# Nine-tap convolution by five products for three outputs in place of four for two, with the first pair's residual rows kept in DRAM

## What is computed

```python
def conv1d_same(x, w, b): ...          # padding SAME along the 748 tokens
rc = conv1d_same(gelu(conv1d_same(xt, rc_w1, rc_b1)), rc_w2, rc_b2)   # router scores, top 2 of 10 experts
y  = ...                               # chosen experts' outputs, weighted by gates
sh = silu(conv1d_same(xt, sh_w1, sh_b1))   # 128 -> 512 channels, NINE taps
sh = conv1d_same(sh, sh_w2, sh_b2)         # 512 -> 128, one tap
z  = residual + y + sh
out = h + layer_norm(z, ln_g, ln_b)
```

## Time and profile before

| | us |
|---|---|
| median of 3 runs | 1531.79 (1531.74 to 1535.3) |
| the profiled execution | 1544.43 |
| its span, first to last instruction | 1542.6 |
| attention, iteration 0 (no convolution), start of `h3` to end of `scores` | 571.5 to 686.6 |
| iterations 1, 2, 3 | 160.8, 163.6, 166.3 |
| the tail, to the first matmul of `experts1` | 1177.3 to 1267.6 |
| PE busy over the span | 1305.9 (85%) |
| the convolution's product matmuls (L1133) | 261.6 busy, 1536 instructions |

### The profile page before, as it was taken

One profiled execution on the slowest core, in us unless ns is written; L12 is line 12 of the kernel. 1 busy time (PEld: TensorE's weight loads), 2 busy tenths in 40 slices (PEclk: granted clock), 3 DMA queues, 4 the chain that ended last, 5 costly groups with the idle time before them and its releaser, 6 DMA issues.

```text
span 1542.6 us, 33397 instructions
## 1 busy us (share of the span) xinstructions
PE 1305.9 (85%) x10360; PEld 1103.2 (72%) x10361; DVE 1003.6 (65%) x3235; ACT 644.9 (42%) x1610; POOL 699.3 (45%) x1055
## 2 busy tenths in 40 slices
PE   6696777787899937778899899988998989999974
PEld 3464646564899935556788778876887989999953
DVE  4467768665466656757863786467663628989946
ACT  1346272523122204335335453445334436666623
POOL 0112556444688853133531444242614526777732
PEclk9697989898999978989999899999998999999987
DMA  6000400003588840010010001000100237777725
GB/s 191 4 21 6 111 27 22 25 21 95 161 266 256 263 170 1 2 42 1 24 61 0 2 14 58 14 1 1 43 1 8 95 97 191 196 194 198 196 88 161
DMA packets 102202, 128.46 MB, mean 83 GB/s; under 512 B 21015, under 2 KB 61181, under 8 KB 101842
## 3 DMA queue, kind: packets, MB, share of 16 engines
q1 hardware_dynamic: 88786, 102.36, 23.1%
...
## 4 chain that ended last, share of the span: by engine, by line
PE 60%; DVE 15%; issue 7%; DVEq 6%; POOL 5%; ACT 4%; DMA 2%; POOLq 0%; SPq 0%; ACTq 0%
PE psum L980 12%; PE psum L1133 11%; PE psum L989 9%; DVE work L1554 3%; PE psum L1142 3%; PE psum L1047 2%; POOL rows_in L2130 2%; PE psum L1094 2%; PE psum L1072 2%; PE psum L794 2%; PE psum L1191 2%; PE psum L969 2%; PE psum L1018 2%; DVE stats L1537 2%; PE psum L1067 1%
## 5 line engine op out<-in xcount | busy, mean ns | idle before, releaser
L1133 PE MATMUL psum<-NT,wreg 128*128 128x182 f32 (+1 forms) x1536 | 261.6, 326 | 10.2 <-ACT pack L1434 5.1
L1133 PEld LDWEIGHTS psum<-NT,wreg 128*128 128x128 f32 x1536 | 247.9, 192 | 18.9 <-ACT pack L1434 5.9
L2162 POOL DMA_INDIRECT rows_out<-work,expert_row_kept x208 | 206.2, 992 | 79.6 <-issue 41.1
L980 PE MATMUL psum<-work 128*128 128x128 f32 x1664 | 222.7, 277 | 0.9 <-ACT work L1336 0.9
L980 PEld LDWEIGHTS psum<-work 128*128 128x128 f32 x1664 | 203.9, 193 | 1.7 <-issue 0.9
L2111 POOL TENSOR_TENSOR rstd<-var_eps,pack 128x6 f32<-128x6 f32 x40 | 56.5, 1415 | 215.0 <-DVE var_eps L1544 214.9
L1329 ACT ACTIVATE work<-psum,work 128x128 f32<-128x128 f32 x416 | 118.6, 368 | 64.4 <-PE psum L980 64.3
L1876 DVE SCALAR_TENSOR_TENSOR work<-psum,work 128x128 f32<-128x128 f32 x416 | 117.1, 344 | 7.7
L794 PE MATMUL psum<-pack,work 128*128 128x128 f32 (+2 forms) x288 | 51.4, 336 | 82.0 <-DVE work L1554 75.5
L1885 DVE TENSOR_SCALAR work<-psum,expert_row_kept 128x128 f32<-128x128 f32 x208 | 72.8, 350 | 71.8 <-PE psum L969 36.6
L2130 POOL DMA_INDIRECT rows_in<-N,slot_now x96 | 100.5, 1046 | 28.6 <-issue 28.4
(11 more groups left out here) (364 smaller groups left out, 2894.3 us busy)
## 6 DMA issues: line engine op xcount, KB each, us to landing
...
```

Source lines behind the costliest of these rows:

```text
L980: r_ = mm(v.ps1[:, c * P:(c + 1) * P], v.w1[:, c * P:(c + 1) * P], v.xT, start=True, stop=True)
L1133: r = mm(bank[:, half * HALF_PAIRS:half * HALF_PAIRS + p1 - p0], weights[:, m * P:(m + 1) * P], product_input(name, g, k, p0, p1), start=( ...
L2162: G.indirect_dma_start(rows_out[m], bass.IndirectOffsetOnAxis(ap=v.dest, axis=0), v.y, None, bounds_check=last, oob_is_err=False).then_inc ...
```

## The change

Three neighbouring outputs of a group now come from five products (points 0 to 4). A unit is a *whole* lane and a block `m`: 250 triples, so 15 matmuls of 250 columns in three fills, `p12` (6), `p03` (6), `p4` (3), where there were 24 matmuls of 192 and 182 columns. The two PSUM banks alternate from fill to fill. DVE joins with 7 operations over 250 columns, SiLU takes 748 columns at once. The four blocks' outputs of a lane no longer fit into their old place: blocks 2 and 3 lie in `H` over the first pair's residual rows, which SP writes to DRAM in iteration 0 and brings back after the second experts' loads. `ln_b` is therefore added earlier, in steps of their own (`add_ln_b`), between `turn(0)` and `add_b_sh2(0)`; `add_b_sh2` adds to `N` alone. `rows` of a lane's two halves now come together: those of lane 0 behind the first unit of lane 1, those of lane 1 both in `CONV_END`. `turn` has 12 additions in place of 3, `make_conv_weights` 8 in place of 3. The weights come by four DMAs in place of two, the same bytes.

```diff
+        CONV_POINTS = 5
+        conv_w = wreg[:, 0:CONV_POINTS * 3 * 512].rearrange("p (x g c) -> p x g c", x=CONV_POINTS, g=3)
...
+        conv_h = [conv_h_own[:, m, :] for m in range(2)] + [
+            H[:, m * TILES:(m + 1) * TILES, :].rearrange("p j d -> p (j d)") for m in range(2)]
+        first_rows = H[:, 0:LANES * TILES, :].rearrange("p j d -> p (j d)")
...
-        for u, (q, m) in enumerate(UNIT):
-            PARTS.append(("bc", q, m))
-            if m == 1 and q > 0:
-                PARTS.append(("rows", q - 1, 0))
-            PARTS.append(("ad", q, m))
-        CONV_END = [("last", UNITS - 1, 3), ("rows", UNITS - 1, 0)]
...
+        for k, m in UNIT:
+            PARTS += [(x, k, m) for x in POINTS]
+            if m == 0 and k > 0:
+                PARTS += [("rows", 2 * k - 2, 0), ("rows", 2 * k - 1, 0)]
+        CONV_END = [("last", LANES - 1, 3), ("rows", UNITS - 2, 0), ("rows", UNITS - 1, 0)]
+        COST = {"p12": 6, "p03": 6, "p4": 3, "rows": 4}
...
+            sp.wait_ge(first_rows_final, 1)
+            sp.dma_start(first_rows_dram, first_rows).then_inc(first_rows_out, 16)
...
+            sp.wait_ge(pe_conv_done, pe_conv.end("conv")[0][1])
+            sp.wait_ge(first_rows_out, 16)
+            sp.dma_start(first_rows, first_rows_dram).then_inc(first_rows_back, 16)
...
+                    for half, x in enumerate(POINTS[what]):
                         for g in range(3):
-                            weights = {"a": conv_taps[:, g, 0], "b": conv_taps[:, g, 1], "c": conv_c[:, g], "d": conv_taps[:, g, 2]}[name]
-                            r = mm(bank[:, half * HALF_PAIRS:half * HALF_PAIRS + p1 - p0], weights[:, m * P:(m + 1) * P],
-                                   product_input(name, g, k, p0, p1), start=(g == 0), stop=(g == 2))
-                    r.then_inc(pe_conv_done, pe_conv.step("conv", f"{what}{m}_{q}", 0))
-                elif what == "rows":
-                    e.wait_ge(act_conv_done, act_conv.at("conv", f"s3_{q}", 0, i))
-                    for j in range(3):
-                        n_ = WIDTH[3 * (q % 2) + j]
-                        acc = conv_bank[1][0:n_, j * P:(j + 1) * P]
-                        for m in range(4):
-                            r = mm(acc, conv_h[:, m, j * P:j * P + n_], conv2[:, m * P:(m + 1) * P], start=(m == 0), stop=(m == 3))
-                    r.then_inc(pe_conv_done, pe_conv.step("conv", f"rows0_{q}", 0))
+                            r = mm(bank[:, half * TRIPLES:(half + 1) * TRIPLES], conv_w[:, x, g, k_cols(m)], turned(k)[:, x, g:g + TRIPLES],
...
+                bk, bm, bi = unit_before(k, m, i, 2 if what == "p12" else 1)
+                e.wait_ge(dve_conv_done, dve_conv.at("conv", f"y{bm}_{bk}", 0, bi))
+                dst = {"p12": conv_p12[u % 2], "p03": conv_p03, "p4": conv_p4}[what]
...
-                V.tensor_tensor(conv_sum[:, 0:n_], b, c, ALU.add)
-                V.tensor_tensor(b, b, c, ALU.subtract)
...
-                V.scalar_tensor_tensor(y[:, 0], conv_sum[:, 0:n_], 0.5, a, ALU.mult, ALU.add)
-                V.scalar_tensor_tensor(y[:, 1], b, 0.5, d_, ALU.mult, ALU.subtract
...
+                if u == 2:
+                    e.wait_ge(first_rows_out, 16)
+                e.wait_ge(act_conv_done, act_conv.at("conv", f"p4{m}_{k}", 0, i))
+                V.scalar_tensor_tensor(conv_sum, p1, 3.0, p2, ALU.mult, ALU.add)
+                V.scalar_tensor_tensor(p2, p1, -3.0, p2, ALU.mult, ALU.add)
+                V.scalar_tensor_tensor(p0, p0, 3.0, p3, ALU.mult, ALU.add)
+                V.scalar_tensor_tensor(conv_p4, conv_p4, 1.5, p3, ALU.mult, ALU.add)
                 e.drain()
-                V.scalar_tensor_tensor(y[:, 0], conv_sum[:, 0:n_], 0.5, a, ALU.mult, ALU.add)
-                V.scalar_tensor_tensor(y[:, 1], b, 0.5, d_, ALU.mult, ALU.subtract
-                                       ).then_inc(dve_conv_done, dve_conv.step("conv", f"y{m}_{q}", 0))
+                V.tensor_tensor(y[:, 0], p0, conv_sum, ALU.subtract)
+                V.scalar_tensor_tensor(y[:, 1], p3, 2.0, p2, ALU.mult, ALU.add)
+                V.scalar_tensor_tensor(y[:, 2], conv_p4, 4.0, conv_sum, ALU.mult, ALU.subtract
...
+            def add_ln_b(k, i, first):
+                e.drain()
+                e.wait_ge(dve_done[k], dve.at("attention", "norm6", k, i))
+                G.tensor_tensor(slots_seen[:], w("nought"), w("nought"), ALU.add)
                 for h, n, tiles in tile_halves(H[:, batch_tiles(i * LANES + k), :]):
-                    G.tensor_tensor(h, h, w("ln_b")[0:n].unsqueeze(1).broadcast_to([n, tiles, P]), ALU.add)
+                    r = G.tensor_tensor(h, h, w("ln_b")[0:n].unsqueeze(1).broadcast_to([n, tiles, P]), ALU.add)
+                if first and k == LANES - 1:
+                    r.then_inc(first_rows_final, 1)
...
-                s = conv_h[:].rearrange("p m c -> p (m c)").rearrange("p (g c) -> p g c", g=3)
-                e.wait_ge(conv_in, 32)
-                G.tensor_tensor(s, conv_taps[:, :, 0], conv_taps[:, :, 2], ALU.add)
+                s = N[:, LANES * TILES:2 * LANES * TILES, :].rearrange("p j d -> p (j d)").rearrange("p (g c) -> p g c", g=3)
+                w0, w1, w2, w3, w4 = (conv_w[:, x] for x in range(CONV_POINTS))
+                e.wait_ge(conv_in, 64)
+                G.tensor_tensor(s, w0, w4, ALU.add)
+                G.tensor_tensor(w3, w1, w1, ALU.add)
                 e.drain()
-                G.tensor_tensor(conv_c, s, conv_taps[:, :, 1], ALU.subtract)
+                G.tensor_tensor(w2, s, w1, ALU.subtract)
+                G.tensor_tensor(w3, w3, w0, ALU.add)
                 e.drain()
-                G.tensor_tensor(conv_taps[:, :, 1], conv_taps[:, :, 1], s, ALU.add)
+                G.tensor_tensor(w1, w1, s, ALU.add)
+                e.drain()
+                G.tensor_tensor(s, w4, w4, ALU.add)
+                e.drain()
+                G.tensor_tensor(s, s, s, ALU.add)
+                e.drain()
+                G.tensor_tensor(w3, w3, s, ALU.add)
...
-                G.tensor_tensor(t[:, 0, :, 0:n], x(0), x(2), ALU.subtract)
-                G.tensor_tensor(t[:, 1, :, 0:n], x(1), x(2), ALU.add)
-                G.tensor_tensor(t[:, 2, :, 0:n], x(2), x(1), ALU.subtract
...
+                G.tensor_tensor(t[:, 3:5], x(3, 2), x(1, 2), ALU.subtract)
+                G.tensor_tensor(t[:, 0], x(0), x(2), ALU.subtract)
+                G.tensor_tensor(t[:, 1], x(1), x(2), ALU.add)
+                G.tensor_tensor(t[:, 2], x(1), x(2), ALU.subtract)
+                e.drain()
+                G.tensor_tensor(t[:, 0], t[:, 0], t[:, 0], ALU.add)
+                G.tensor_tensor(t[:, 1], t[:, 3], t[:, 1], ALU.subtract)
+                G.tensor_tensor(t[:, 2], t[:, 2], t[:, 2], ALU.add)
+                G.tensor_tensor(t[:, 4], t[:, 4], t[:, 3], ALU.subtract)
+                e.drain()
+                G.tensor_tensor(t[:, 0], t[:, 0], t[:, 3], ALU.add)
+                G.tensor_tensor(t[:, 2], t[:, 2], x(3), ALU.add)
+                G.tensor_tensor(t[:, 4], t[:, 4], t[:, 3], ALU.subtract)
+                e.drain()
+                G.tensor_tensor(t[:, 2], t[:, 2], x(2), ALU.subtract
...
                 turn(0, i)
+                add_ln_b(0, i, first)
+                add_ln_b(1, i, first)
                 add_b_sh2(0, i)
```

More of the change, by code:

```diff
@@ L581, in interleaved @@
             order, n, reached = [], 0, 0
+            costs = [COST[x] for x, *_ in PARTS]
             for x in range(ATT_STEPS * LANES):
@@ L584, in interleaved @@
                 reached += FILL[x // LANES]
[L585 removed]
+                while conv and n < len(PARTS) and sum(costs[:n]) * sum(FILL) * LANES < reached * sum(costs):
                     order.append(("conv", n, 0))
```

196 lines of the change are left out of this document (108 added, 88 removed).

## The result

The changed kernel takes **1623.7 us** (median of four runs, 1615.1 to 1625.0) against 1532.17 of the old one beside it: a ratio of 1.058, interval 1.054 to 1.062. The forecast was 1597 within 1562 to 1622, so the direction holds, and the time lies 1.7 us beyond the range's upper end (by the ratio, against the 1531.79 that the forecast started from, it is 1620.8, just inside). Of the 91.5 us that the change costs, the forecast had 65. The profiled execution took 1624.96 (span 1622.8), 80.5 more than that of before.

What follows compares the result with a forecast made beforehand. PE was taken to bound the kernel, busy 95 to 99% outside the boundary, with waits for in-order POOL outweighing its saving. Iterations 4.9 and 41.4, weights 15, tail 3, loads 1: +65 on the 1531.79 median, 1597, range 1562 to 1622 us.

Steps and rivals of the forecast that it cites:

- PE's saving: Product matmuls: 120 of 425 ns replace 192 shorter ones per iteration, 10 us less for each of four pairs, 41 in all.
- (a): From `out` to `norm6T`: POOL reaches `rstd` 6 late, behind both rows and the scatters; 29.0 us for 18.4, +10.6.
- (b): Rest of an iteration: q, k, v +1.9, chunk steps -7, `norm6T` to `scores` -0.6, together -5.7 us.
- PE hides it: Chunk steps: PE's work covers DVE's join, grown from 4 operations to 7, so the stage gives its 7 us.
- (c): Boundary, `scores` to `norm5T` of lane 1: POOL's two longer `turn`, 7.7 us each, in the chain; +15.8 at two steady boundaries.
- R3: Rival: DVE and POOL hold each other; boundaries and tail 2.5 to 5 us more each, weights 5; 1615; chance 0.13.
- (d): Boundary before the first convolution: POOL is not behind there and DVE is the limit; change 0.
- (e): Convolution weights in iteration 0: five more POOL additions hold DVE; +15 us, between nothing and 17.
- (f): Tail, 90.3 us before: the chain sums to 91, DVE held once by `turn(1)` +2; taken as +3, bounds 0 and +8.
- (g): Residual rows out and back, and weight loads in pieces of 2 KB: rows covered by other work, weights +1 us.
- R4: Rival: residual rows' copy out delays the third join, or their copy back the output; 1605; chance 0.65 together with the forecast.
- R2: Rival: one of the two waits is mostly covered by work left over, 25 to 30 us less; 1570; chance 0.14.

Runs made afterwards that it cites:

- x1: The changed kernel with lane 1's scatters and rstd 6 of both lanes ahead of the first rows' additions on POOL: 1711.9 us beside an old kernel of 1669.3.
- x2: The changed kernel with turn(0), both add_ln_b and add_b_sh2(0) ahead of add_conv_rows(2) on POOL: ratio 1.007 to the old kernel.
- x9: The changed kernel with turn cut from twelve additions to two, POOL's order kept, the convolution's output being other numbers: ratio 1.005 to the old kernel.
- x4: The changed kernel with make_conv_weights cut from eight POOL additions to three, the convolution's products being other numbers: ratio 1.025 to the old kernel.
- x3: The changed kernel with the POOL moves of both x1 and x2, run twice: ratios 1.013 and 1.022 to the old kernel.
- the second group: The unaltered changed kernel again (ratio 1.057) and three altered versions of it, run beside an old kernel of 1532.1 us.

## Why the prediction was right, and where not

**PE's saving** held as worked out: 90 instructions, 45 matmuls, of the tail take 19.14 us, 425 ns each.

**(a)** held nearly to the tenth: forecast 29.0, measured 28.87, by the mechanism named, and x1 took it away (12 us, 14.4 to 3.3 of waiting).

**(b)** failed in one step, "PE hides it". q, k, v took a little more than forecast (+2.5 for +1.9) and the last stage gave more (-1.9 for -0.6), but the chunk steps gave back 4.0, 2.5 and 5.2 in the three iterations, not 7 each. With fewer products between the steps, PE waits 6.9 us there for DVE where it waited 4.7, 3.1 and 4.7. PE's timeline, then DVE's:

```profile
947.05 1.14 PE L1075 MATMUL psum<-work 64*128 64x256 f32 x8 [1.32 <-DVE work L1988]
...
955.52 0.43 PE L1095 MATMUL psum<-work 128*32 128x128 f32 x8 [3.41 <-DVE work L1961]
...
966.33 0.43 PE L1095 MATMUL psum<-work 128*32 128x128 f32 x8 [1.20 <-DVE work L1961]
```

```profile
949.28 0.22 DVE L1725 COPY N<-N 128x120 f32<-128x120 f32 x1
...
954.17 2.35 DVE L1961 TENSOR_TENSOR work<-psum,pack 128x1024 f32<-128x1024 f32 x2
```

I had read PE's 95% as room for the whole saving, and had looked only at DVE's join. But the join isn't the largest part. The wait of 3.41 us ends at L1961, which DVE reaches after 4.9 us of slot computation for the scatters (L1725 to L1767, from 949.28). Before the change the same place cost 2.84, 1.24 and 2.85 in the three iterations, of which the second is

```profile
915.77 0.43 PE L1067 MATMUL psum<-work 128*32 128x128 f32 x8 [1.24 <-DVE work L1934]
```

Another 2.3 us are the attention's own steps (L1988), where it was 0.8 before in the same iteration. Only the 1.20 stands behind a join of seven operations. What the chunk steps fell short, 3.0, 4.5 and 1.8 us, comes to 9.3, more than the whole 8.8 by which the iterations without their boundary exceed the forecast.

**(c)** was right in mechanism (x2 and x9 each take 12 to 13 off) and low by 3.0 each time: the two `turn` took 10.0 and 9.6 us for the 7.7 taken, beyond the upper bound of 9.0, which is 4.2 in all; the rest of the chain was 1.1 shorter than its sum. 8.7 of each is its own, since additions of 252 columns cost 0.6 to 0.8 each, far from proportional to their columns. The other 1.3 and 0.9 are R3.

**(d)** was off by 2.0 in the good direction. **(e)** had the right place and too high a price: 8.8 for 15 (x4). **(f)** had +3 for 7.5. x2, which takes 11.4 off the tail, shows `turn(0)` on its path, and that came at 20.1 us for 19. From there to the first `rows` it took 40.8 us for the 34.2 of the sum. PE never waits for `turn(1)` itself, but once for a bank:

```profile
1295.41 14.50 PE L1169 MATMUL psum<-NT,wreg 128*128 128x250 f32 x60 [3.28 <-ACT conv_p L1473]
```

ACT's copy ahead of it waited for DVE's second join. The first, beside `turn(1)`, took 5.7 us (1279.12 to 1284.82) where the third takes 2.7, which the prediction had as +2; between them DVE did 7.2 us of slot computation (L1720 to L1767), for which it had no term. No run took that away, so it is read from the trace alone. **(g)** The start differs by 13 us among profiles of kernels that are alike up to there (570.1 to 583.2 in before, after and the second group), so the +4.1 can't be put down to the weights' pieces. The third join never waits for the copy of the rows, and experts and output are level: R4 didn't come.

Some luck is in the total: the stretches that came longer than forecast did so by 23 us, and (d) and (e), which came shorter, hid 8 of them.

**R3**, at 0.13, is real and smaller than its price: POOL's `turn` is stretched from 8.7 to 10.0, and DVE is held far more than POOL (the join at the boundary takes 6.4 us, from 897.41, where one alone takes 2.7). In `turn(0)` it isn't the join, as R3 had it, but two DVE operations of 768 and 640 columns at 878.39 and 880.41, beside which two additions take 1.33 and 1.19. The Trainium skill (GPSIMD Engine Reference, section Key points) has both share their SBUF interfaces, with contention where a VectorE instruction has two SBUF inputs or runs in a 2-port mode; here the trace agrees, in both directions, with 5.81 us for 1.63 on DVE's side and 10.0 for 8.7 on POOL's. `norm6`, which took the 5.81, reads one SBUF tile and two scalars a row, so what I had taken from the page, two inputs, isn't the whole of it; the trace doesn't show the mode. The Trainium skill's 2.6 cycles a column (same page, section Elementwise) come to 7.1 us for the 3276 columns of `turn`. The "nearly 9" of the prediction adds about 0.15 for each of the 12 additions, a dispatch that the section prices for VectorE and not for GpSimd, so that it came near the 8.7 is luck. **R2**, that one wait would cover the other, is out: both stood in full, and the boundary gives its 12 to 13 us with or without the other move (x2, x3).

**From the profile to the median.** The terms come to 65.3 and the profiled executions differ by 80.5. The other 11 of the miss is no term: I took 12.6 off because the old kernel's profiled run lay that far above its median, and the changed one's lies 1.3 above. Why the one was long stays open; the start's spread of 13 us could hold it, but nothing here shows that.
